# Decoder layer on Trainium2: ScalarE's first root and silu ahead of the spread copy, half of batch 2's output products in scan slots

## What is computed

```
x = x + attention(layernorm(x))        # 16 heads, 2 KV heads, causal; output product Wo, bias bo
x = x + mamba(ctx, z=layernorm(x))     # conv, selective scan over 512 steps; y * silu(z)
x = x + ffn(layernorm(x))              # router top 2 of 16 experts, relu^2 experts, plus a shared relu^2 FFN
```

## Time and profile before

| | us |
|---|---|
| median of 3 runs (1140.94 to 1142.09) | 1141.82 |
| the profiled execution: its time | 1142.33 |
| its span | 1140.6 |
| mean granted TensorE clock | 0.986 |
| PE busy | 1072.7 (94%) |
| DVE busy | 827.3 (73%) |
| ACT, POOL busy | 677.0, 676.1 (59% each) |

### The profile page before, as it was taken

The page is one execution under the profiler, slowest core; times in us unless marked ns, Lnnn a source line. Parts: engine busy times, 40 slices in busy tenths (PEclk is TensorE's granted clock), DMA queues, the critical chain, the costliest instruction groups (busy, mean ns, idle before and its releaser), DMA issues.

```text
span 1140.6 us, 19239 instructions
## 1 busy us (share of the span) xinstructions
PE 1072.7 (94%) x6714; PEld 671.2 (59%) x6714; DVE 827.3 (73%) x1245; ACT 677.0 (59%) x1466; POOL 676.1 (59%) x587
## 2 busy tenths in 40 slices
PE   8999988889999999999998999899999999999993
PEld 3554456666666666666666554444444477777761
DVE  6988699999999999999999966830680144433438
ACT  4876789999999999999999835312011022323220
POOL 2012399999999999999999834102043045555530
PEclk9999989999999999999999999999999999999997
DMA  7210001112111121111221043112225534344329
GB/s 222 93 39 20 21 28 38 38 36 69 38 31 36 29 75 32 35 31 36 84 70 34 11 162 135 74 37 74 76 76 200 182 89 136 129 139 131 71 79 386
DMA packets 51983, 94.77 MB, mean 83 GB/s; under 512 B 9966, under 2 KB 18158, under 8 KB 51888
## 3 DMA queue, kind: packets, MB, share of 16 engines
q1 hardware_dynamic: 44368, 72.82, 19.6%
q0 software_dynamic: 7520, 20.72, 5.9%
HBM read 74.51 MB, written 20.84 MB: 84 GB/s over the span
## 4 chain that ended last, share of the span: by engine, by line
PE 68%; DVE 10%; ACT 8%; POOL 7%; issue 6%; DMA 1%; SPq 0%; DVEq 0%; POOLq 0%; ACTq 0%
PE ps L1558 9%; PE ps L1985 7%; PE ps L1997 7%; PE ps L829 6%; POOL w_all L763 5%; PE ps L857 4%; PE ps L1572 4%; PE ps L818 4%; PE ps L803 4%; PE ps L356 4%; DVE w_all L1041 3%; PE ps L308 3%; PE ps L1581 2%; ACT w_all L955 2%; PE ps L868 2%
## 5 line engine op out<-in xcount | busy, mean ns | idle before, releaser
L763 POOL TENSOR_TENSOR w_all<-w_all 128x512 f32<-128x512 f32 x256 | 322.7, 1288 | 20.2 <-DVE w_all L585 14.8
L1041 DVE TENSOR_TENSOR_SCAN w_all<-ps,w_all 128x512 f32<-128x512 f32 x256 | 298.7, 1205 | 1.2 <-POOL w_all L763 0.6
L938 ACT ACTIVATE ps<-w_all,low 128x512 f32<-128x512 f32 x256 | 177.6, 697 | 1.0 <-DVE w_all L1041 0.8
L857 PE MATMUL ps<-ident,w_all 128*128 128x128 f32 x1024 | 162.0, 281 | 9.6 <-DVE acc L1049 9.4
L946 ACT ACTIVATE w_all<-ps,low 128x128 f32<-128x128 f32 (+3 forms) x256 | 133.1, 531 | 13.6 <-DVE low L1033 13.6
L857 PEld LDWEIGHTS ps<-ident,w_all 128*128 128x128 f32 x1024 | 114.9, 142 | 34.6 <-issue 20.8
L955 ACT ACTIVATE w_all<-ps 128x256 f32<-128x256 f32 (+2 forms) x192 | 102.0, 531 | 22.6 <-PE ps L818 22.3
L2035 DVE COPY attn<-w_all 128x512 f32 x94 | 40.0, 428 | 103.8 <-PE ps L1985 103.0
L1033 DVE TENSOR_REDUCE low<-ps 128x2 f32<-128x256 f32 (+3 forms) x128 | 103.8, 811 | 14.6 <-PE ps L803 14.0
L1558 PE MATMUL ps<-w_all 128*128 128x512 f32 x256 | 112.2, 594 | 0.0
L818 PE MATMUL ps<-ident,w_all 128*128 128x128 f32 x640 | 108.8, 285 | 1.5 <-ACT low L961 1.5
(11 more groups left out here) (223 smaller groups left out, 1703.9 us busy)
## 6 DMA issues: line engine op xcount, KB each, us to landing
w_all<-b_scratch SPq DMA_DIRECT2D x64, 256.0 KB, 3.3
w_all<-in_w_up SPq DMA_DIRECT2D x16, 512.0 KB, 5.4
w_all<-in_w_down SPq DMA_DIRECT2D x16, 512.0 KB, 6.2
w_all<-sorted_y SPq DMA_DIRECT2D x16, 512.0 KB, 10.5
norms<-attn SPq DMA_DIRECT2D x4, 1024.0 KB, 4.3
out_dram<-acc SPq DMA_DIRECT2D x16, 256.0 KB, 9.0
attn<-in_x SPq DMA_DIRECT2D x3, 1024.0 KB, 6.1
attn<-in_x SPq DMA_DIRECT2D x12, 256.0 KB, 4.6
```

What stands on the lines that cost most here:

```text
L763: pool.tensor_tensor(dbu[:, k, :], keep["du"][i // N][:, k * T:(k + 1) * T], b_all[i % 2][:, :], ALU.mult).then_inc(pool_dbu.sem, pool_dbu ...
L857: last = pe.transpose(yb[which][:, k * P:(k + 1) * P], state[i % 2][:, k, t * P:(t + 1) * P], ident[:, :])
L938: act.activation(da[unit % 2][:, :], keep["dt"][i // N][:, k * T:(k + 1) * T], ACT.Exp, scale=keep["a_flat"][:, unit % (N * KD):unit % (N ...
L1041: dve.tensor_tensor_scan(state[i % 2][:, k, :], da[unit % 2][:, :], dbu[:, k, :], 0.0, ALU.mult, ALU.add).then_inc(dve_scan.sem, dve_scan. ...
```

## The change

It touches the order of three engines and one bound.

- `HALVES` becomes 20: four more half-width products, those of batch 2's row tiles 0 and 1, in slots 102, 106, 110 and 114. `project_tail` keeps tiles 2 and 3 alone: 8 wide matmuls in banks 0 and 1.
- ACT leaves the last spread copy to `close`: the order `copy_tail(0), copy_tail(1), spread copy, root(0), silu(0), copy_tail(2), copy_tail(3)` becomes `copy_tail(2), root(0), silu(0), spread copy, copy_tail(3)`.
- Batch 3's products use the banks in the order 2, 3, 0, 1 and are made in the order of tiles 2, 0, 1, 3; `add_last` follows as 2, 3, 0, 1, and DVE's `first_stats(1, ...)` all come behind `add_last(3)`, `copy_logits(0)` behind `normalize_z(1)`.
- PE: `turn_z(2, 2)`, `turn_z(3, 0)` and `turn_z(3, 2)` each go about one `down` later. DVE: `normalize_z(3)` ahead of `gate(2)`, `base(0, 0)` and `base(0, 1)` earlier, `copy_logits(1)` ahead of `gate(3)`. ACT: roots and silus of batches 2 and 3 in another order among the `relu`s.

The diff, cut (before.py to after.py):

```diff
-    HALVES = 2 * NT * TAIL
+    HALVES = 2 * NT * TAIL + NT
...
         project_tail(3, 4)
         turn_prob(UNITS - 2, 1)
         turn_state(UNITS - 1, 0)
-        project_tail(4, 6)
+        project_tail(4, 5)
         weigh_v(UNITS - 2)
...
-        project_tail(6, 8)
+        project_tail(5, 6)
         turn_prob(UNITS - 1, 1)
-        project_tail(8, 10)
+        project_tail(6, 7)
         weigh_v(UNITS - 1)
         spread(spread_in(UNITS + 2))
-        project_tail(10, 4 * KD)
+        project_tail(7, 8)
...
             first_deviation(0)
             silu(0)
-            scan["copy_tail"](act, 2)
+            scan["copy_spread"](act, UNITS // 8 - 1)
             scan["copy_tail"](act, 3)
...
-            project_out(0, 3)
+            project_out(2)
+            project_out(0)
+            project_out(1)
             turn_n(0, 0)
             turn_n(0, 2)
-            project_out(3, 4)
+            project_out(3)
...
             turn_n(1, 0)
-            turn_z(2, 2)
...
             down(0, 0)
             turn_n(1, 2)
-            turn_z(3, 0)
+            turn_z(2, 2)
             down(0, 1)
             logits(1)
-            turn_z(3, 2)
+            turn_z(3, 0)
             down(0, 2)
             turn_logits(1)
+            turn_z(3, 2)
             turn_n(2, 0)
             down(0, 3)
...
             scan["normalize"](dve, UNITS // 8 - 1)
-            first_stats(1, 0, 1)
             gate(0)
             normalize_n(0)
-            add_last(0, 2)
-            first_stats(1, 1, 4)
+            add_last(2)
+            add_last(3)
+            first_stats(1, 0, 4)
             aggregate(1)
+            add_last(0)
+            normalize_z(1)
             copy_logits(0)
-            normalize_z(1)
...
-            base(0, 0)
+            base(0, 1)
+            copy_logits(1)
             gate(3)
-            copy_logits(1)
-            base(0, 1)
             add_logits(1)
```

More of the change, by code:

```diff
@@ L873, in project_tail @@
             for n in range(first, end):
-                t, k = n // KD, n % KD
+                t, k = 2 + n // KD, n % KD
                 if n == 0:
                     pe.wait_ge(act_p.sem, act_p.upto(2 * UNITS - 1))
-                if n == 2 * KD:
-                    pe.wait_ge(dve_scan.sem, dve_scan.upto(2 * UNITS - 1))
-                last = pe.matmul(bank[t], keep["attn"][:, TAIL, k * T + t * P:k * T + (t + 1) * P], keep["wo"][:, k, :],
+                last = pe.matmul(bank[t - 2], keep["attn"][:, TAIL, k * T + t * P:k * T + (t + 1) * P], keep["wo"][:, k, :],
                                  start=(k == 0), stop=(k == KD - 1))
                 if k == KD - 1:
-                    last.then_inc(pe_out.sem, pe_out.tick(HALVES + t))
+                    last.then_inc(pe_out.sem, pe_out.tick(HALVES + t - 2))
         pe.wait_ge(first["q"].sem, first["q"].upto(4 * (B - 1) + 1))
@@ L957, in spread @@
         def spread(quad):
[L958 to L961, removed]
+            copy_spread(act, quad)
         def weigh_c(n):
@@ L992, in scalar @@
                 weigh_c(g - 2)
-            if spread_in(g) is not None:
+            if spread_in(g) is not None and g < UNITS + 2:
                 spread(spread_in(g))
@@ L1010, in scalar, with copy_spread @@
             if g == UNITS + 1:
-                copy_tail(act, 0)
-                copy_tail(act, 1)
+                copy_tail(act, 2)
+    def copy_spread(act, quad):
+        act.wait_ge(pe_turn.sem, pe_turn.upto(turn["r", quad]))
+        if quad >= 1:
+            act.wait_ge(dve_out.sem, dve_out.upto(quad - 1))
+        act.activation(r_all[:, :], tb[:, :], ACT.Copy).then_inc(act_turn.sem, act_turn.tick(turn["r", quad]))
     def copy_tail(act, t):
-        act.wait_ge(pe_out.sem, pe_out.upto(HALVES + t))
-        act.activation(x1[TAIL][:, t, :], bank[t], ACT.Copy).then_inc(act_out.sem, act_out.tick(HALVES + t))
+        act.wait_ge(pe_out.sem, pe_out.upto(HALVES + t - 2))
+        act.activation(x1[TAIL][:, t, :], bank[t - 2], ACT.Copy).then_inc(act_out.sem, act_out.tick(HALVES + t - 2))
     def residual(dve, b, t):
@@ L1069, in mix @@
     return {"sync": sync, "gpsimd": gpsimd, "tensor": tensor, "scalar": scalar, "vector": vector,
-            "residual": residual, "res": dve_res, "xb": pool_xb, "with_bias": with_bias, "bias_at": bias_at, "copy_tail": copy_tail, "out_done": act_out, "last_out": last_out, "normalize": normalize, "acc": dve_acc, "pool_acc": pool_acc, "out": dve_out, "y": pe_y, "pv": pe_pv, "p": act_p, "s": pe_s,
+            "residual": residual, "res": dve_res, "xb": pool_xb, "with_bias": with_bias, "bias_at": bias_at, "copy_tail": copy_tail, "copy_spread": copy_spread, "out_done": act_out, "last_out": last_out, "normalize": normalize, "acc": dve_acc, "pool_acc": pool_acc, "out": dve_out, "scan": dve_scan, "y": pe_y, "pv": pe_pv, "p": act_p, "s": pe_s,
             "cy": act_cy, "turn": act_turn, "rinv": dve_rinv}
@@ L1392, in close @@
         pe_late, act_first = signal("pe_late"), signal("act_first")
+        last_bank = [bank[2], bank[3], bank[0], bank[1]]
+        last_at = {2: 0, 0: 1, 1: 2, 3: 3}
         def down_bank(b, t):
@@ L1508, in _, with project_out @@
             scan["tensor"](pe)
-            def project_out(first, end):
-                for t in range(first, end):
+            def project_out(t):
+                if t >= 2:
                     pe.wait_ge(scan["out_done"].sem, scan["out_done"].upto(scan["last_out"](LAST - 1, t)))
-                    for k in four:
-                        last = pe.matmul(bank[t][:, :], attn[:, LAST, k * T + t * P:k * T + (t + 1) * P], wo[:, k, :], start=(k == 0), stop=(k == 3))
-                    last.then_inc(pe_wo.sem, pe_wo.tick(t))
+                else:
+                    pe.wait_ge(scan["scan"].sem, scan["scan"].upto(2 * UNITS - 1))
+                for k in four:
+                    last = pe.matmul(last_bank[t][:, :], attn[:, LAST, k * T + t * P:k * T + (t + 1) * P], wo[:, k, :], start=(k == 0), stop=(k == 3))
+                last.then_inc(pe_wo.sem, pe_wo.tick(last_at[t]))
             def turn_z(b, first):
@@ L1704, in _ @@
             silu(1)
-            relu(0, 1, 3)
+            relu(0, 1, 2)
             first_deviation(2)
+            relu(0, 2, 3)
             silu(2)
@@ L1709, in _ @@
             second_deviation(1)
-            relu(0, 5, 7)
+            relu(0, 5, 8)
             first_deviation(3)
-            relu(0, 7, 8)
+            silu(3)
             turned(1, 0)
+            turned(1, 2)
             second_deviation(2)
-            silu(3)
-            turned(1, 2)
             second_deviation(3)
@@ L1742, in acc, with add_last @@
                 return keep["acc"][:, b, t * D:(t + 1) * D]
[L1744 to L1748, removed]
+            def add_last(t):
+                dve.wait_ge(pool_xb.sem, pool_xb.upto(scan["bias_at"](LAST, t)))
+                dve.wait_ge(pe_wo.sem, pe_wo.upto(last_at[t]))
+                dve.tensor_tensor(x1[LAST][:, t, :], last_bank[t][:, :], x1[LAST][:, t, :], ALU.add).then_inc(dve_x1.sem, dve_x1.tick((t + 2) % 4))
             def first_stats(b, first, end):
@@ L1752, in first_stats @@
                     if b == LAST:
-                        dve.wait_ge(dve_x1.sem, dve_x1.upto(t))
+                        dve.wait_ge(dve_x1.sem, dve_x1.upto((t + 2) % 4))
                     else:
@@ L1829, in _ @@
             gate(1)
-            add_last(2, 4)
+            add_last(1)
             normalize_n(1)
@@ L1833, in _ @@
             aggregate(3)
+            normalize_z(3)
             gate(2)
-            normalize_z(3)
+            base(0, 0)
             normalize_n(2)
-            base(0, 0)
+            base(0, 1)
+            copy_logits(1)
             gate(3)
-            copy_logits(1)
-            base(0, 1)
             add_logits(1)
```

2 lines of the change are left out of this document (1 added, 1 removed).

## The result

The changed kernel takes 1145.61 us (median of 6 runs, 1143.93 to 1146.6), the kernel before 1141.91 in the same comparison: a ratio of 1.0039, with a 95% interval of 1.0027 to 1.0051. The forecast was 1141.1 us, 1138.4 to 1143.9, and "no difference that can be told". It is wrong by 4.5 us; the runs show a slowdown of 3.7 us, and the chance given to that was 0.10. The profiled execution took 1146.1 us, 3.8 more than that of before.

A forecast was written before the change was run, and what follows sets the result against it. PE was taken to bound the kernel behind the scan, all four engines being full within it. A +2.3, B -7.2, D +1.8, E -5.4, F +7.8 sum to -0.7 us, giving 1141.1 us, range 1138.4 to 1143.9.

The forecast's parts named there:

- A: Scan: four more half-width products in slots cost +2.3 us, all exposed since all engines are full there; ends 0 and 6.9.
- B: Tail behind the scan: eight wide products fewer and an earlier silu(0) bring `turn_z(0, 2)` forward, -7.2 us; ends -7.0 to -7.5.
- C: PE's clock behind the tail's two new short waits: it may hold or fall as before, 0 or -1.7 us.
- D: New PE wait at `turn_logits(0)`, as batch 1's statistics and the logit copy follow PE's last product: +1.8 us; ends 0 and 2.8.
- E: PE's waits of 1.69 and 2.05 us at the moved `turn_z` vanish: -3.7 us, and -1.7 for the clock.
- F: New PE wait of 6.7 us at `turn_n(2, 0)` for the logit sum behind gate(3): +6.1 us, and +1.7 for the clock.
- the two short waits: PE's pair of 1.6 and 1.0 us at `turn_z(0, ...)` and 1.8 us at `turn_logits(0)`; one was forecast to lower the clock.
- the one that ended slower: Long wait at `turn_n(2, 0)` keeps the clock low for some 9 us or more: +2.7, 1144.5 us; chance 0.06.

The follow-up runs named there:

- f_split: Changed kernel with DVE's logit sum add_logits(1) moved between the second and third product of gate(3): 1136.92 us, ratio 0.995 to the kernel before.
- d_copy: Changed kernel with DVE's copy_logits(0) straight behind aggregate(1), ahead of add_last(0) and normalize_z(1): 1142.55 us, ratio 1.0013 to the kernel before.
- b_pool: Changed kernel with POOL's bias additions for batch 3 waiting until DVE has normalized all of z(0): 1141.65 us, ratio 0.9995 to the kernel before.
- all3: Changed kernel with POOL's additions behind normalize_z(0), copy_logits(0) ahead of normalize_z(1), and add_logits(1) inside gate(3): 1130.83 us, ratio 0.9897 to the kernel before.
- act_only: Kernel before with only ACT's root(0) and silu(0) put ahead of the last spread copy: 1137.89 us, ratio 0.9966.
- scan_only: Kernel before with only four more half-width products in scan slots and eight wide ones fewer in the tail, ACT's spread copy still first: 1142.40 us, ratio 1.0004.

## Why the prediction was wrong

Its terms against the steps of the table:

| term | forecast | measured | |
|---|---|---|---|
| A, four products in scan slots | +2.3 | +2.9 | 2.3 in the scan, 0.6 ahead of it |
| B, the tail to `turn_z(0, 2)` | -7.2 | -4.7 | mis-sized |
| C, the clock behind B | 0 or -1.7 | +1.3 | wrong sign; 0 in f_split and d_copy |
| D, `turn_logits(0)` | +1.8 | +2.6 | mis-sized, inside its ends |
| E, the waits of 1.69 and 2.05 us with their clock | -5.4 | -6.0 | right; 0.6 more than summed, not traced |
| F, `turn_n(2, 0)` with its clock | +7.8 | +7.7 | right |

- **B failed at one step**: "The same form takes 2.97 us in place of 1.92 beside POOL's squares; the last silu comes about 0.4 later". I saw that POOL's additions would lie beside the normalization, and priced the meeting by a row in which POOL worked beside DVE for 1.8 of 2.97 us. POOL's squares there, in the kernel before:

```profile
718.49 2.22 POOL L1491 TENSOR_TENSOR w_all<-w_all 128x512 f32<-128x512 f32 x2 [6.01 <-ACT w_all L1693]
```

Here POOL had four additions in a row, two of which wait for silu(0) and so came early with it, and DVE's instructions came at POOL's pace to the end: 5.16 us. From root to last silu it was 6.4 us where the sum has 3.8 and 0.4. The bound from the trace of before would have been four instructions at POOL's 1.25 us, 5.0; "Ends: -7.0 to -7.5" left it out. b_pool shows it: without the meeting `turn_z(0, 2)` starts 17.2 us behind the tail's start, 24.5 before, so B is -7.3, as forecast; all3 has the same 17.2.
- **C** followed from it in part. The clock fell behind the wait of 3.68 us in all three profiles that have it (the changed kernel, f_split, and d_copy with 3.67), and stayed up in the two with B at its forecast size (b_pool, all3): there the optimistic half of "0 or -1.7" was right. But how much it costs is not set by the wait: B and C together are -3.4 us in the changed kernel's profile and -4.8 in f_split's and d_copy's, after the same idle time and on the same code. That difference of 1.4 us stays open. b_pool comes nearest to what the forecast described, B as summed and one of the two short waits lowering the clock, and took 1141.65 us against its 1141.1. The Trainium skill (TensorE: Matmul & The Clock Gate, "Why this matters for your kernels") warns only of gaps longer than the 2.63 us of before. That agrees with the clock at 1.00 behind 1.10 and 0.88 us and with 3.68 and 6.41 us lowering it, but not with 2.05 and 2.63 us before, nor with the waits of 2.48 us in f_split and 2.47 in b_pool.
- **D**: named at its place and with its cause. I took normalization as 1.92 us; `normalize_z(1)` met POOL's first square (1.28 us from 697.86) and took 2.63. It is the same mechanism as B, and its end of 2.8 held it.
- **F** decided most, as the text said, and f_split shows the mechanism alone: the logit sum behind gate(3), whose third product waits for the transposes that stand just before. The wait was 6.41 us where 6.7 was forecast.
- **E** and **A** held: no wait at the two moved `turn_z`, and 2.3 us for the four slots, with a period of 32.2 us where two of them lie.
- **The rivals**: the one that ended slower was the wrong mechanism. The clock stayed low for 3.8 us behind the long wait, not for the 9 us from which that rival would decide. In the profile, the 4.5 us above the forecast are B's 2.5, the clock's 1.3, D's 0.8 and the 0.6 ahead of the scan, less 0.6 for E and 0.1 for F. No rival joined them.

## What to carry to other kernels

When an edit lets an engine start early, look at what the others run at that new moment, not only at what it waited for: here four VectorE normalizations from SBUF to SBUF beside four GpSimd additions ran at GpSimd's pace, and a bound for such a meeting is count times that pace. A transpose that feeds a long chain must have cover between itself and the next instruction that needs the chain's end; moving it "one product later" can move it behind its last cover, and a small piece taken out of the chain (here the logit sum) is as good as moving it back. Try such a change in parts: ACT's order alone gave 3.9 us, the moved transposes gave 6 and cost 8 by the steps of the trace (no run moved them alone), and with three small repairs the same change is 11 us faster than the kernel before instead of 4 slower.

## What the runs showed of the hardware

- Four normalizations of 128x512 f32 from SBUF to SBUF (one tensor operand) take 1.92 us alone, 2.22 to 2.97 beside one or two POOL instructions, and 5.16 beside four. Each side slows: POOL's four took 5.51 us, 4.96 when they ran beside products that read PSUM. The four statistics (BATCH_NORM_STATS2) took 2.46 us with POOL's addition running beside the last of them, as alone.
- The same idle time of PE, 2.47 or 2.48 us, left the clock at 1.00 in one profile and lowered it in two others; 2.05 us lowered it in all three profiles that have it (before, act_only, scan_only). 1.69 us never did in the same three, nor 1.10 and 0.88 us with transposes between in b_pool and all3. A forecast can only give such a wait of 2 to 2.5 us a chance of costing 1.7 us more.
- How long the clock is low, counted from where PE resumes, did not follow from the idle time: 3.3 us behind 2.63, 3.8 behind 6.41 in the changed kernel, and behind 3.68 us 5.2 in f_split and 5.1 in d_copy; in the changed kernel 5.9 from the second transposes on, which followed 3.68 and 0.89.
- The clock also differs between executions of one kernel. Of 19 runs of the kernel before, four took 1138.73 to 1139.49 us at a mean granted clock of 0.990 to 0.992; the profiled one took 1142.33 at 0.986. So the clock terms read from one profile are those of one execution. No trace of such a quick run was kept.
